# Moving two layer norms of the next token group into the previous group, and four buffers instead of two for the first layer norm

## The reference

```python
x = x + _layernorm(attn(_layernorm(x)))          # one head of 1024, softmax over keys,
                                                 # out = einsum('bqk,bqd->bkd', weights, v)
xt = _layernorm(x)
scores = softmax(xt @ gate_w.T)                  # 16 experts, fp32
c      = scores where expert is in the best 2 of 4 groups and in the best 4, else 0
h1 = einsum('td,edi->tei', xt, w1); h3 = einsum('td,edi->tei', xt, w3)
y  = einsum('tei,eid,te->td', silu(h1) * h3, w2, c)
z  = silu(xt @ ws1) * (xt @ ws3) @ ws2           # shared expert
x  = x + _layernorm(y + z)
```

## Time and profile before

| what | us |
|---|---|
| runs: median (lowest to highest) of 3 | 5355.84 (5211.28 to 5638.55) |
| profiled execution, time | 5202.51 |
| profiled execution, span of the slowest core | 5201.0 |
| PE busy (share of the span) | 4165.5 (80%) |
| DVE busy | 2018.8 (39%) |
| ACT busy | 856.4 (16%) |
| POOL busy | 84.6 (2%) |

### The profile page before, as it was taken

The page is one execution under the profiler, slowest core; times in us unless marked ns, Lnnn a source line. Parts: engine busy times, 40 slices in busy tenths (PEclk is TensorE's granted clock), DMA queues, the critical chain, the costliest instruction groups (busy, mean ns, idle before and its releaser), DMA issues.

```text
span 5201.0 us, 53881 instructions; the slowest of 8 cores (5176.5 to 5201.0 us)
## 1 busy us (share of the span) xinstructions
PE 4165.5 (80%) x18864; PEld 1938.5 (37%) x18864; DVE 2018.8 (39%) x3050; ACT 856.4 (16%) x1332; POOL 84.6 (2%) x42
## 2 busy tenths in 40 slices
PE   3679857677799699969954679799979969996995
PEld 2334323232444344434422234344444434443442
DVE  2323533333433443443352323533343344344335
ACT  2114122222111111111102124111111111111110
POOL 0000000000000000000010000000000000000001
PEclk7889968888899799979976789899979979997997
DMA  3000358888344334334433100434333433433442
GB/s 122 29 13 5 138 195 282 280 283 281 118 150 148 128 124 160 116 128 154 156 106 119 33 9 29 151 129 147 137 122 146 154 122 126 158 115 128 154 155 104
DMA packets 123565, 695.63 MB, mean 134 GB/s; under 512 B 9620, under 2 KB 9620, under 8 KB 86440
## 3 DMA queue, kind: packets, MB, share of 16 engines
q1 hardware_dynamic: 123304, 692.18, 37.9%
HBM read 601.96 MB, written 90.18 MB: 133 GB/s over the span
## 4 chain that ended last, share of the span: by engine, by line
PE 69%; DVE 11%; DMA 11%; issue 4%; ACT 2%; POOL 1%; DVEq 1%; SPq 0%; ACTq 0%; POOLq 0%
PE PS L33 69%; DMA RV<-w 5%; DVE RA L33 3%; DVE st L33 2%; DVE RK L33 2%; DMA RV<-x1park 2%; DMA RK<-x 2%; POOL RV L33 1%; DVE c_buf L33 1%; DVE glog L33 1%; DVE RW L33 1%; ACT RK L33 1%; DVE RV L33 1%; DMA RA<-Wq 1%; DMA RA<-Wv 1%
## 5 line engine op out<-in xcount | busy, mean ns | idle before, releaser
L33 PE MATMUL PS<-RQ,RW 128*128 128x512 bf16 x9216 | 2070.1, 386 | 153.4 <-DVE RK L33 76.1
L33 PEld LDWEIGHTS PS<-RQ,RW 128*128 128x128 bf16 x9216 | 913.5, 99 | 1285.4 <-issue 236.6
L33 PE MATMUL PS<-RW,RK 128*128 128x512 bf16 x4608 | 1079.8, 392 | 277.4 <-DVE RA L33 266.8
L33 DVE SCALAR_TENSOR_TENSOR RA<-PS,c_buf,RA 128x1024 f32<-128x1024 f32 x480 | 614.7, 1283 | 1035.7 <-PE PS L33 1035.1
L33 PEld LDWEIGHTS PS<-RW,RK 128*128 128x128 bf16 x4608 | 444.8, 100 | 890.2 <-issue 439.8
L33 ACT ACTIVATE RK<-PS 128x512 f32<-128x512 f32 (+1 forms) x608 | 370.5, 620 | 2355.4 <-PE PS L33 2343.9
L33 DVE TENSOR_TENSOR RK<-RK,PS 128x512 bf16<-128x512 f32 x576 | 394.4, 688 | 488.4 <-PE PS L33 483.8
L33 PE MATMUL PS<-identb,RA 128*128 128x128 bf16 x640 | 73.4, 292 | 336.1 <-DVE RA L33 324.8
L33 PE MATMUL PS<-RV,RA 128*128 128x512 bf16 x1024 | 228.3, 383 | 24.6 <-ACT RV L33 13.6
L33 PE MATMUL PS<-RA,RW 128*128 128x512 bf16 x1024 | 238.7, 398 | 8.5 <-DVE RA L33 8.5
L33 PE MATMUL PS<-RK,RQ 128*128 128x512 bf16 x1024 | 221.3, 379 | 3.0 <-DVE RV L33 3.0
(11 more groups left out here) (73 smaller groups left out, 1554.9 us busy)
## 6 DMA issues: line engine op xcount, KB each, us to landing
RW<-wbf SPq DMA_DIRECT2D x126, 2048.0 KB, 7.7
RW<-wbf SPq DMA_DIRECT2D x126, 1024.0 KB, 6.0
RV<-w SPq DMA_DIRECT2D x96, 1024.0 KB, 7.5
wbf<-RW SPq DMA_DIRECT2D x18, 2048.0 KB, 13.9
wbf<-RW SPq DMA_DIRECT2D x18, 1024.0 KB, 8.1
RA<-x SPq DMA_DIRECT2D x32, 512.0 KB, 3.3
RK<-x SPq DMA_DIRECT2D x32, 512.0 KB, 4.2
x1park<-RK SPq DMA_DIRECT2D x32, 512.0 KB, 2.9
```

The lines of the kernel that those rows point to most:

```text
L33: self._last = getattr(self.e, name)(*a, **k)
```

## The change

A1 gets four buffers each for `xstage` and `xnbf`, so that a load of x waits for the layer norm four tiles before instead of two; the squares of the layer norm get one buffer instead of two, and the regions are laid out anew in RA (`xnTc` now lies where the cast weights of A0 lay). `back_kb` is cut in two: `back_ln` (load and layer norm) and `back_tr` (transposes, copies, gate matmuls, logits). For the entry of group 0 the two are called so that a tile's layer norm stands two tiles ahead of its transposes. For groups 1 to 3, `back_ln` of the first two tiles is called in the group before, behind `unit_sv` of unit 12; the group starts with `back_tr` of these two, then come `back_ln` of the last two and `back_tr` of the last two.

```diff
-        xstage = RA[:, 4096:6144]
-        xnbf = RAb[:, 12288:14336]
-        sqA1 = RA[:, 7168:9216]
-        bvrep = RA[:, 9216:10240]
-        xnTc = RAb[:, 20480:24576]
+        xstage = RA[:, 4096:8192]
+        xnbf = RAb[:, 16384:20480]
+        sqA1 = RA[:, 10240:11264]
+        bvrep = RA[:, 11264:12288]
+        xnTc = RAb[:, 0:4096]
...
-                            q.wait(mget(f"T{gti - 2}ln"))
+                            q.wait(mget(f"T{gti - 4}ln"))
...
-                                pre_s=[f"T{gti - 2}tp"])
+                                pre_s=[f"T{gti - 4}tp"])
...
-                def back_kb(kb, b=b):
+                def back_ln(kb, b=b):
                     def bk_d(q, b=b, kb=kb):
                         q.wait(mget(f"b{b}k{kb - 2}gtr"))
...
                     mput(f"b{b}k{kb}xn2ln", mget(f"b{b}k{kb}x1ln"))
 
+                def back_tr(kb, b=b):
                     def bk_t(t, b=b, kb=kb):
...
                 for g in range(NCH):
+                    if g == 0:
+                        back_ln(0)
+                        back_ln(1)
+                        back_tr(0)
+                        back_ln(2)
+                        back_tr(1)
+                        back_ln(3)
+                        back_tr(2)
+                        back_tr(3)
                     if g > 0:
                         def yprev(t, b=b, g=g):
                             unit_y(t, g * NPE - 1)
                         pr.on("t", yprev)
                         unit_stt(g * NPE - 1)
-                    for kb in range(4 * g, 4 * g + 4):
-                        back_kb(kb)
+                        back_tr(4 * g)
+                        back_tr(4 * g + 1)
+                        back_ln(4 * g + 2)
+                        back_ln(4 * g + 3)
+                        back_tr(4 * g + 2)
+                        back_tr(4 * g + 3)
                     gate_group(g)
...
                         unit_sv(u)
+                        if e == 12 and g + 1 < NCH:
+                            back_ln(4 * (g + 1))
+                            back_ln(4 * (g + 1) + 1)
```

## The result

The profiled execution of the changed kernel took 5162.66 us (span 5161.1), where the forecast was 5162 and the kernel before took 5202.51. Timed against each other, the ratio of changed to before is 0.9917, with a 95% interval from 0.9902 to 0.9933: faster by 0.83%, about 43 us, with an interval that does not reach 1. The plain medians, 5309 of 5318 us over ten runs each, say less, since both contain executions in which one half of the chip ran slower; the ratio leaves those out.

A forecast was written before the change was run, and what follows sets the result against it. PE bounds steady groups; group changes wait on layer norms and ACT's order, the first group on weight loading. Gains 71.6 less costs 20.0 and 11.3 give -40.3: 5202.5 to 5162 us; own range 5148 to 5179, stated 5125 to 5215, upper end carried to 5325.

The forecast's parts named there:

- same: Whole kernel: time within 2% (104 us) of before, taken as what a measurement can tell; chance 0.94.
- the hoist that eats the gain: Rival at unit 12's stt: pair uncovered, 14.3 us per steady group, decisive from 12.1; 5213 us, chance 0.09.
- Groups 2 and 3: Four changes of group: earlier first transpose and new order end the last gate 12.2 us sooner each, 48.8 together.
- Group 1: Two changes to group 1, no output tiles in front: last gate 8.9 us earlier each, 17.8 together.
- Group 0: Two entries of group 0, only ACT's order changes: last gate 2.5 us earlier each, 5.0 together.
- The pair in a steady group: Two moved layer norms at unit 12: 10.9 us against 7.95 idle on DVE; with clock 4.0 each, five groups 20.0.
- The table switch: ACT's table load at each hoist: 1.28 us taken; rival at about 2.66 gives 5169 us, chance 0.05.
- The weight-loading group: Group 0 of batch 0: pair stands ahead of DVE's cast in unit 13, loads hidden; costs 11.3 us.
- The clock as a rival: Group changes: four tiles at 2.4 GHz give 5096 us, only the first two 5129; chance 0.11.
- Only the first layer norm is saved: Rival at group changes: tiles keep 9.07 us spacing through another ACT wait; gain 47 us, 5187 us, chance 0.12.

The follow-up runs named there:

- stay: Split kernel, but in batch 0's weight-loading group the first two layer norms of group 1 stay at that group's start; profiled execution 5146.83 us.
- Split: Changed kernel with the two moved layer norms one by one, behind units 12 and 13, instead of both behind 12; ratio 0.9875, profiled 5150.87 us.
- third: Changed kernel with a third layer norm, of no use, behind unit 12; profiled execution 5208.69 us.
- filled: Split kernel, but in the weight-loading group the two layer norms stand between DVE's three casts of unit 13; ratio 0.9862, profiled 5148.06 us.

## Why the prediction was right in its parts, and the step that failed

The step that failed is the last: the chances. Forecast 5162, range 5125 to 5325, and all of it bound to a threshold of 2%, so that "same" got 0.94. The runs tell 0.16% to either side, and by them the kernel is faster (0.9917). By the prediction's own cases all but the hoist that eats the gain, 0.91, ended under the kernel before by more than that. No step of the mechanism lay behind this; the scatter that I had in view was that of the three runs shown, and not of comparisons between like executions.

That the profiled time came within 1 us of the forecast is luck: the interval allows a gain of 35 to 51 us, and in the profiled executions the gains were 3.5 us above the sum and the first stretches 6.3 us longer, for which the sum had nothing.

- *Groups 2 and 3.* Right in cause and nearly in size: 11.9 to 13.8 us for 12.2. The square root of the fourth tile ahead of the third's copies showed as forecast. Two errors in the walk partly offset each other. The start, 8.5 us earlier in the forecast, was read off core 3, where the first transpose stood 8.92 us behind the last `stt`; by the median of the cores that was 6.6 to 8.7 us, now 0.15. And the four tiles are 5.6 to 6.1 us shorter (medians), where the forecast had 3.7: the first tile's transposes took 1.06 us instead of 1.94. The clock was at its upper level for one tile, behind 1.55 us of idle time, in all 48 changes of group; behind the 7.93 us of stay, and behind 7.1 us or more in the kernel before, they took 1.94.
- *Group 1.* 9.5 and 10.7 us for 8.9; the first tile's clock again.
- *Group 0.* 2.2 and 2.4 for 2.5.
- *The pair in a steady group.* 2.8 us of gap plus the clock's drop in 21 of 40: 3.6 in the mean over all cores, 4.0 forecast. "Split" shows that DVE's idle time is what covers, "third" that beyond it all falls on PE.
- *The table switch.* The trace has 1.68 against 0.40 us again at the moved layer norms, so 1.28 for a switch and nothing behind it. Back to silu the first activation starts right behind the load too (1634.42 + 1.28, then 1635.71). The Trainium skill's 2.66 us ("ScalarE: Activation LUTs", "What ACT_TABLE_LOAD costs") does not show in these rows. To break the rule of the Trainium skill's same page ("Rules for kernel authors"), all work of one table before a switch, cost PE nothing here: the split kernel switches twice as often in that place, and its units are at 20.8 us.
- *The weight-loading group.* 12.0 for 11.3, of which "filled" gives back about 8, the order on DVE, and leaves 4, about 3 of them the loads, where I had all of it on DVE and the loads hidden. In the changed kernel they are hidden, so the sum came out.
- *The clock as a rival* was right in kind for one tile and no further: in the stretch of the four tiles the granted clock was 0.59, where the four tiles of the earlier trace rows had 0.50.

```profile
1767.00:1795.00 28.00, 18.43 (x94) 17.06 (x94) 8.34 (x17) 8.99 (x21) 0.00 (x0) 0.59 0.68 264
```

- *Only the first layer norm is saved*, and *the hoist eats the gain*: neither came; the second tile's transpose has no wait, and the price per steady group is 3.6 and not 12.1 us.

## What to carry to other kernels

Before work is moved under a saturated engine, measure the idle time of the engine that is to do it at the very place in its order, and cut the work to pieces that fit: one layer norm of 6.1 us in 7.95 us was free, two cost 3.6 us, three 10. A stage with another bound (here the loading of weights) needs its own sum, and there the same move was a loss, 6.8 us gained for 12 to 15. And when a change is forecast to be small, compare it to the scatter between like executions, not to that of a list of runs.

## What the runs showed of the hardware

A gap of 2.71 us on a busy PE was followed by a drop of the granted clock in 21 cases of 40, and one of 7.49 to 7.85 us in 40 of 40; the drop cost 1.3 to 1.7 us behind the former (24.9 to 25.3 less 23.6) and 1.6 to 2.7 behind the latter (5.2 to 6.3 for 16 matmuls that take 3.6). Behind a gap of 1.49 us 32 matmuls took their 7.07 us, and behind 1.55 us the first tile's transposes ran at the upper level in all 48 changes. POOL's additions beside the steady units, 9.4 us per group, cost PE nothing.
